# Sending the row of maxima from ScalarE's queue instead of SyncE's in a two-layer windowed attention kernel

## The reference

```
x = x + attention(groupnorm(x))        # 32 groups, 12 heads of 16 channels
attn = (q * scale) k^T + rel_h[query, key row] + rel_w[query, key column]
out  = softmax(attn) v @ proj_w + proj_b
```

## Time and profile before

| | |
|---|---|
| median of 3 runs | 2341.02 us (2326.52 to 2341.86) |
| the profiled execution | 2339.97 us, span 2338.2 us |
| granted TensorE clock, mean | 0.978 |
| busy: PE, DVE, ACT, POOL | 90%, 71%, 69%, 31% |
| DMA | 216.34 MB, mean 93 GB/s |

### The profile page before, as it was taken

How to read it: one execution, slowest core, us unless ns; L and a number is a source line. 1 busy time by engine, 2 the same in 40 slices (tenths; PEclk the granted TensorE clock), 3 DMA queues, 4 the chain that set the end, 5 groups by cost and what they waited for, 6 DMA issues and landing times.

```text
span 2338.2 us, 73485 instructions
## 1 busy us (share of the span) xinstructions
PE 2094.7 (90%) x27904; PEld 1595.9 (68%) x27904; DVE 1653.4 (71%) x3923; ACT 1621.4 (69%) x3713; POOL 714.4 (31%) x1796
## 2 busy tenths in 40 slices
PE   1899999999999989999999999899989999999998
PEld 1677676776767767667667766677766766777765
DVE  5677777667767677777677777677767777777675
ACT  0577777677767667767676777677767776777675
POOL 1233323333333233333233333233223333333230
PEclk9899999999999999999999999999999999999999
DMA  1333434333434333433333443344334343334331
GB/s 47 84 94 95 104 91 105 91 92 91 103 93 97 90 94 93 101 93 93 91 98 91 94 103 96 88 96 100 91 91 102 94 100 93 94 93 103 91 92 47
DMA packets 170550, 216.34 MB, mean 93 GB/s; under 512 B 29783, under 2 KB 138072, under 8 KB 170202
## 3 DMA queue, kind: packets, MB, share of 16 engines
q1 hardware_dynamic: 170202, 211.64, 37.7%
HBM read 117.00 MB, written 57.80 MB: 75 GB/s over the span
## 4 chain that ended last, share of the span: by engine, by line
PE 39%; DMA 33%; SPq 14%; DVE 6%; issue 4%; ACT 3%; POOL 1%; POOLq 0%; ACTq 0%; DVEq 0%
PE ps_m L412 18%; DMA q_st<-mrow 17%; DMA k_dram<-qk_hl 10%; PE ps_sc L538 7%; PE ps_max L525 6%; SPq L375 6%; DMA q_dram<-qk_hl 6%; DVE qk_hl L734 4%; PE ps_o L557 3%; SPq L382 3%; ACT qk_hl L598 2%; SPq L341 2%; SPq L387 2%; PE ps_m L501 2%; DVE rel_hl L776 1%
## 5 line engine op out<-in xcount | busy, mean ns | idle before, releaser
L722 DVE TENSOR_REDUCE mx<-ps_max 98x2 f32<-98x392 f32 x1536 | 819.4, 562 | 232.6 <-PE ps_max L525 215.5
L586 ACT ACTIVATE probs<-ps_sc 98x392 f32<-98x392 f32 x1536 | 714.5, 497 | 232.3 <-PE ps_sc L538 198.2
L525 PE MATMUL ps_max<-k_st,q_st 124*98 124x196 f16 x3072 | 548.9, 261 | 82.4 <-DVE mx L722 82.1
L538 PE MATMUL ps_sc<-q_st,k_st 125*98 125x196 f16 x3072 | 523.3, 252 | 95.6 <-DMA q_st<-mrow 94.1
L776 DVE TENSOR_TENSOR rel_hl<-ps_m,rel_hi 64x504 f16<-64x504 f32 (+1 forms) x768 | 431.4, 562 | 162.0 <-ACT rel_hi L643 152.9
L525 PEld LDWEIGHTS ps_max<-k_st,q_st 124*98 124x98 f16 x3072 | 295.0, 126 | 296.4 <-issue 198.0
L538 PEld LDWEIGHTS ps_sc<-q_st,k_st 125*98 125x98 f16 x3072 | 320.9, 126 | 123.1 <-DMA q_st<-mrow 120.4
L557 PE MATMUL ps_o<-probs,v_st 98*32 98x196 f32 x6144 | 389.6, 340 | 0.5 <-ACT o_sb L578 0.5
L634 ACT ACTIVATE rel_hi<-ps_m,is_lo 64x504 f16<-64x504 f32 (+1 forms) x384 | 223.9, 583 | 189.1 <-PE ps_m L471 185.7
L471 PE MATMUL ps_m<-q_st,rel_st 64*32 64x84 f16 x7168 | 341.6, 266 | 4.8 <-DVE rel_hl L776 4.5
L809 POOL TENSOR_TENSOR msq<-mv 96x2 f32<-96x2 f32 x128 | 24.4, 191 | 1007.1 <-DVE mv L748 1007.1
(11 more groups left out here) (72 smaller groups left out, 3293.8 us busy)
## 6 DMA issues: line engine op xcount, KB each, us to landing
q_st<-q_dram SPq DMA_DIRECT2D x128, 294.0 KB, 3.8
k_st<-k_dram SPq DMA_DIRECT2D x256, 147.0 KB, 3.9
q_dram<-qk_hl SPq DMA_DIRECT2D x128, 147.0 KB, 2.6
k_dram<-qk_hl SPq DMA_DIRECT2D x128, 147.0 KB, 2.7
q_st<-rel_hl SPq DMA_DIRECT2D x256, 73.5 KB
q_st<-rel_hl SPq DMA_DIRECT2D x256, 64.3 KB
xa<-in_x SPq DMA_DIRECT2D x64, 147.0 KB
xd<-in_x SPq DMA_DIRECT2D x64, 147.0 KB
```

What stands on the lines that cost most here:

```text
L525: last = nc.tensor.matmul(ps_max[head % 2][0:HT, h * TOK:h * TOK + TOK], q_st[u.r][0:R_MAX, head, h, :], k_st[u.r][0:R_MAX, head, :], star ...
L538: last = nc.tensor.matmul(ps_sc[head % 2][0:HT, kt * TOK:kt * TOK + TOK], k_st[u.r][0:STACK, head, kt * HT:kt * HT + HT], q_st[u.r][0:STAC ...
L586: nc.scalar.activation(probs[head][:, :, :], ps_sc[head % 2][0:HT, 0:2 * TOK].rearrange("p (k t) -> p k t", k=2), ACT.Exp, scale=1.0 / (QS ...
L722: nc.vector.reduce_max(mx[u.r % 2][:, head, :], ps_max[head % 2][0:HT, 0:2 * TOK].rearrange("p (q k) -> p q k", q=2), axis=AX.X).then_inc( ...
```

## The change

The two sends of a unit move from SyncE's program to ScalarE's. `SEND_LATER` counts from the place of TensorE's transpose, as `ACT_LATER["mT"]` does, which is also 1. The transfers, their semaphores and everything else stay.

```diff
-        SP_AT = {"m0": 39, "m1": 46, "rel": 22, "qk_out": 3, "q_in": 3, "k_in": 4, "xd": 55, "out": 69, "xa": -12}
+        SEND_LATER = 1
+        SP_AT = {"rel": 22, "qk_out": 3, "q_in": 3, "k_in": 4, "xd": 55, "out": 69, "xa": -12}
...
-            def maxima(unit_, half):
-
-                if active(unit_):
-                    wait(sp, s_mrow, unit_.n * 2 + half + 1)
-                    sp.dma_start(q_st[unit_.r][R_MAX:STACK, half * HH:half * HH + HH, :, :],
-                                 mrow[unit_.r % 2][:, half, :]).then_inc(s_m[half][unit_.r], 16)
-
...
             def iteration(unit, layer):
                 for s in range(HEADS):
-                    for half in range(2):
-                        u = due(unit, s, SP_AT[f"m{half}"])
-                        if u:
-                            maxima(u, half)
...
                             nc.scalar.activation(mrow[u.r % 2][:, half, :], ps_m[BANK[name]][0:HEADS, 0:HT],
                                                  ACT.Copy, scale=-1.0 / KS).then_inc(s_mrow, 1)
+                    for half in range(2):
+                        u = due(unit, s, AT[f"mT{half}"] + SEND_LATER)
+                        if u:
+                            act.wait_ge(s_mrow, u.n * 2 + half + 1)
+                            act.dma_start(q_st[u.r][R_MAX:STACK, half * HH:half * HH + HH, :, :],
+                                          mrow[u.r % 2][:, half, :]).then_inc(s_m[half][u.r], 16)
```

## The result

The changed kernel takes 2523.74 us (median of 4 runs, 2505.23 to 2535.98) against 2337.26 of the kernel before: ratio 1.080, 95% interval 1.071 to 1.089. It is 8% slower; the forecast was 2381 us with a range to 2440. The profiled execution took 2535.98 us, its span is 2534.2.

What follows compares the result with a forecast made beforehand. TensorE, busy 90% of the span, was taken as the bound, standing 94.1 us before the scores matmul for the row-of-maxima transfer. Sum: 2340 - 94 + 102 + 17 + 16 (queues issuing at once) = 2381 us, range 2300 to 2440.

Steps and rivals of the forecast that it cites:

- (f): TensorE's clock: half-clock stretches going with long DMA waits set against the new slot-8 wait; 0, between -25 and +80 us.
- (a): Half 1's row of maxima leaves early, so TensorE's whole DMA wait before the scores matmul goes: -94 us.
- (b): ScalarE held 0.80 us issuing half 1 in slot 6, delaying o_sb and TensorE in slot 8: +102 us.
- (c): ScalarE issuing half 0 in slot 0, mostly within slack, delays TensorE 0.13 us a unit: +17 us.
- (e): SyncE loses two issues per unit, but its next transfers wait for their data, so nothing comes earlier: 0.
- rival of a falling clock: Clock falls where ScalarE is waited for, or issues pile up; every second unit at 1.2 us: 2458 us, chance 0.13.

Runs made afterwards that it cites:

- sp_early: Kernel before with both sends kept on SyncE, half 1's moved from slot 10 to slot 4, ahead of the k_st loads: 2200.0 us, ratio 0.936.
- half1_only: Changed kernel with only half 1 sent by ScalarE, directly behind its row; half 0 sent by SyncE as before: 2466 us, ratio 1.056.
- half0_only: Changed kernel with only half 0 sent by ScalarE, directly behind its row; half 1 sent by SyncE as before: 2366.1 us, ratio 1.013.
- send_later2: Changed kernel with SEND_LATER = 2, both sends still on ScalarE but placed later in its program: 2205.4 us, ratio 0.937.

## Why the prediction was wrong

Its direction was right, and so were the waits that it named; one term, (f), the clock, was mis-sized by some 160 us.

- **(a), the early send, -94 us:** right. The wait went from 94.1 to 1.0 us. What it is worth in all is more: sp_early is 137 us under 2337, because the half-clock stretches behind the long waits (busy time 2094.7 to 2043.0 us, 52) go with it.
- **(b), ScalarE held, half 1, +102, and (c), half 0, +17:** right in place and size. The issue took 726 ns at the median (I took 730), the hold was 0.78 us (0.80), and line 491 is where TensorE waits; the weight-load side stood 96.2 us there, the matmul side, whose ends are modelled, 69.8. The units at full clock show both terms apart. From one start of line 491 to the next they take, at the median, 16.36 us in sp_early, 17.17 in half1_only and 17.30 in the changed kernel: 0.81 us for half 1 and 0.13 for half 0, as forecast. With the clock kept up by extra matmuls the changed kernel stands at 2309 to 2312, that is 109 to 112 us over sp_early, for the 119 of (b) and (c).
- **(e), 0:** right.
- **(f), the clock, 0, between -25 and +80:** wrong, and it is the step that failed. I set the stretches that would go against those that would come and let them cancel. Measured: old ones gone, about -52 us; new ones +212 us (2524 against 2312 with the waits filled); in all +160, and 2340 - 94 + 102 + 17 + 160 = 2525. I had written that the new wait stands next to the one of 0.71 us, "some 1.5 us of standing within 2", and had a row in which the clock fell behind a long DMA wait; what I failed to weigh is that this pair of waits comes in each of 128 units. The clock then fell in 82 of them, where in the kernel before it fell in 17, and it cost up to 2.9 us each time (20.20 against 17.30).
- The Trainium skill, "DMA: Bandwidth & Descriptors", section "Issuing engines are not separate DMA queues", says that issuing from several engines saves only the time to start a transfer. As a bound of the gain that is too small for this kernel: the early send saves the whole wait of 94 us. That a second issuing engine brings nothing else agrees with the runs: sp_early gets the same from SyncE's own queue by another order.

The rival of a falling clock, which had a chance of 0.13 and a price of 2458, is what came, at 2524. Its count, every second unit, was not far off (64 against 82); its price for one, 1.2 us against up to 2.9, was the larger error, since it was taken from the v step alone.

What stays open: why half0_only is 1.3% and not 0.7% slower. Its profiled execution is only 10.7 us over that of before, and of that 13.2 us are matmul busy time. Open too is what decides in which units the clock falls: units with nearly the same waits do and don't have it.

## What to carry to other kernels

An engine that waits for its own last result before it issues a DMA is held for the whole issue; with one instruction of work between the two, the issue hides under it (2466 against 2211 us). Before adding a wait of half a microsecond to TensorE, look at what other wait stands beside it in the same stretch: here the clock was lost on the two together, and it cost twice what the new wait did (212 us against some 100). And where a transfer leaves late, look first at what it is queued behind: one number in SyncE's order gave 6.5%.

## What was not expected of the hardware

- The clock answers steeply. Holding ScalarE 0.68, 0.78 and 0.93 us in each unit gave mean granted clocks of 0.980, 0.926 and 0.894, with a fall in 10, 53 and 78 of 127 units.
- Two waits of about 0.64 and 0.55 us, with some 0.5 us of work between them, come in every unit of the changed kernel, and in 82 of 127 the clock falls from 2.4 to 1.2 GHz, so that its mean is 0.89; with the wait for o_sb or that for the maximum filled it is 0.997 or 0.991.
- In send_later2 a DMA issue in ScalarE's stream is handled ahead of compute instructions that stand before it in the program and have not begun (1103.87 against 1104.49). It leaves 0.04 us after the semaphore wait of the last instruction in front of it is fulfilled (scores matmul ended 1103.83), though its own row was ready at 1103.07.
